# Seven slots for the spread C rows, extra TensorE products in two pauses, and last outputs in four banks

## What is computed

```python
# 1: c = x W + (x A_id) B_id
xp = c @ x_proj_w.T                        # 32 columns of dt_in, 16 of B, 16 of C
dt = softplus(dt_in @ dt_proj_w + dt_proj_b)
dA, dBx = exp(dt[..., None] * A), dt[..., None] * B * c[..., None]
h = dA_t * h + dBx_t                       # the scan over 64 steps, 16 states per feature
y = einsum('bdn,bn->bd', h, C_t)           # the states times C, summed over the 16 states
x = x + y + D * c
# 2: v = x W2 + bias + adapter;  logits = v @ router_w.T;  top 2 of 4 experts, softmax
x = x + gates * ((v @ A_e) @ B_e)          # "out": the last product, rank 64 to 1024 columns
```

## Time and profile before

| | us |
| --- | --- |
| median of 3 runs | 905.21 |
| the 3 runs | 905.06, 905.21, 910.86 |
| the profiled execution's own time | 910.61 |
| its span, first to last instruction | 908.40 |
| mean granted TensorE clock in the span | 0.968 of full |

### The profile page before, as it was taken

One profiled execution on the slowest core, in us unless ns is written; L12 is line 12 of the kernel. 1 busy time (PEld: TensorE's weight loads), 2 busy tenths in 40 slices (PEclk: granted clock), 3 DMA queues, 4 the chain that ended last, 5 costly groups with the idle time before them and its releaser, 6 DMA issues.

```text
span 908.4 us, 18640 instructions
## 1 busy us (share of the span) xinstructions
PE 808.6 (89%) x6416; PEld 770.8 (85%) x6416; DVE 764.3 (84%) x688; ACT 641.4 (71%) x1489; POOL 689.0 (76%) x349
## 2 busy tenths in 40 slices
PE   5999999999898989899987997889998999688784
PEld 4988998899888988899987997889987999577672
DVE  3447789989989898988997897989999799989993
ACT  4556778787677876787785875878777786768750
POOL 2015788898779886898887885889879888789791
PEclk9996999999999999999998999999999999789998
DMA  9988687575647667475647556485665653243211
GB/s 247 384 327 276 224 238 212 165 246 160 221 123 259 192 199 218 157 231 167 234 136 247 177 158 214 118 266 172 212 192 179 224 167 129 73 146 97 87 64 47
DMA packets 103113, 172.24 MB, mean 190 GB/s; under 512 B 21865, under 2 KB 71657, under 8 KB 94830
## 3 DMA queue, kind: packets, MB, share of 16 engines
q1 hardware_dynamic: 85614, 94.12, 34.7%
q10 hardware_dynamic: 17408, 76.95, 24.3%
HBM read 137.33 MB, written 33.69 MB: 188 GB/s over the span
## 4 chain that ended last, share of the span: by engine, by line
PE 56%; ACT 11%; DVE 10%; issue 8%; POOL 7%; DMA 5%; SPq 1%; POOLq 0%; ACTq 0%; DVEq 0%
PE jb L1047 25%; PE yp L1214 14%; PE dBx L1047 8%; DVE h L1011 6%; POOL hC L578 6%; ACT dA L612 6%; PE jb L1051 4%; PE yp L1047 3%; DMA stacked<-dtx_scratch 3%; POOL dtx L558 2%; DMA dtx_scratch<-HL 1%; DMA x<-in_x 1%; PE yp L1051 1%; DVE HL L906 1%; DVE Bd L829 1%
## 5 line engine op out<-in xcount | busy, mean ns | idle before, releaser
L578 POOL TENSOR_TENSOR hC<-h,Cb 128x1024 f32<-128x1024 f32 (+1 forms) x256 | 634.6, 2482 | 145.5 <-DVE h L1011 128.7
L1011 DVE TENSOR_TENSOR_SCAN h<-dA,dBx 128x1024 f32<-128x1024 f32 x256 | 583.2, 2280 | 67.8 <-PE dBx L1047 58.0
L612 ACT ACTIVATE dA<-dt,negA 128x252 f32<-128x252 f32 x1024 | 430.2, 494 | 75.2 <-DVE h L1011 64.9
L1214 PE MATMUL yp<-ident,hC 128*128 128x128 f32 x2048 | 274.9, 278 | 25.9 <-DVE dt L813 14.1
L1214 PEld LDWEIGHTS yp<-ident,hC 128*128 128x128 f32 x2048 | 237.0, 144 | 30.8 <-POOL hC L578 20.0
L1047 PE MATMUL jb<-xT,Wst 128*128 128x256 f32 x1416 | 213.9, 293 | 4.4 <-DVE dt L813 4.4
L1047 PE MATMUL dBx<-Bd,stacked 96*128 96x256 f32 x1024 | 187.3, 306 | 20.8 <-DMA stacked<-dtx_scratch 11.1
L1047 PEld LDWEIGHTS jb<-xT,Wst 128*128 128x128 f32 x1416 | 183.5, 192 | 7.1 <-DVE dt L813 5.2
L1047 PEld LDWEIGHTS dBx<-Bd,stacked 96*128 96x128 f32 x1024 | 147.3, 196 | 27.3 <-issue 24.4
L558 POOL TENSOR_TENSOR dtx<-dt,u 128x256 f32<-128x256 f32 x64 | 53.3, 834 | 40.0 <-DVE dt L813 40.0
L647 ACT ACTIVATE u<-jb 128x512 f32<-128x512 f32 x31 | 18.5, 598 | 41.1 <-PE jb L1047 38.7
(11 more groups left out here) (173 smaller groups left out, 721.7 us busy)
## 6 DMA issues: line engine op xcount, KB each, us to landing
Wst<-W_scratch ACTq DMA_DIRECT2D x54, 1024.0 KB, 5.7
stacked<-dtx_scratch SPq DMA_DIRECT2D x192, 128.0 KB, 2.7
dtx_scratch<-HL SPq DMA_DIRECT2D x64, 256.0 KB, 3.4
Cb<-c_scratch SPq DMA_DIRECT2D x32, 512.0 KB, 6.0
xres<-in_x SPq DMA_DIRECT2D x64, 128.0 KB, 3.9
out<-obuf SPq DMA_DIRECT2D x32, 256.0 KB, 3.3
xin<-in_x ACTq DMA_DIRECT2D x26, 256.0 KB, 5.0
GB<-in_L_cond_lora_B SPq DMA_DIRECT2D x64, 64.0 KB, 5.6
```

Of the source, the lines that this page charges most:

```text
L578: pool.tensor_tensor(*(x[:, :, ns, :] for x in times_C(un)), ALU.mult).then_inc(hC_made, 1)
L612: act.activation(dA[:, half % NDA, :].rearrange("p (b n t) -> p b n t", b=GB_, n=HS)[:, :, n, 1:STEPS], dt[:, j % NDT, :].rearrange("p (b ...
L1011: dve.tensor_tensor_scan(h[:, un % NH, :], dA[:, half % NDA, UNIT * p:UNIT * (p + 1)], dBx[un % 2][:, :], 0.0, ALU.mult, ALU.add).then_inc ...
L1214: last = pe.matmul(y, hC[:, un % NHC, P * n:P * (n + 1)], ident[:, :], is_transpose=True, start=un == 0 and n == 0, stop=False, skip_group ...
```

## The change

1. `Cb` gets seven slots in place of four. Unit un of group G lies in slot (4 G + un) mod 7. Where before the four spreads of a group were issued in (7, 1), (7, 2), (7, 3) of the group before and (0, 1) of its own, now two are issued in (6, 3), one in (7, 0) and one in (7, 1). The wait ahead of one is for the product that used the slot seven units' worth of C earlier.
2. A new helper `keep_clock(psum, n)` issues n products of 128 x 512 columns on `expBT` whose results nobody reads: 8 behind the setup, 9 ahead of gm and 2 behind it in the tail.
3. The eight products of the last group's outputs go into the four banks of `dBx`, in another order: both first products of outputs 0 and 1 need gm's high part alone, and the wait for the low part stands behind them. The additions are made in place in `x1`, and the last group's stores read from there; there is no wait for `out_done`.
4. A scratch of the program for software-made DMA descriptors goes from 1024 to 512 bytes.

```diff
+SPREAD = {(6, 3): (0, 1), (7, 0): (2,), (7, 1): (3,)}
-        Cb = sb("Cb", [P, UNITS, UNIT])
+        Cb = sb("Cb", [P, NCB, UNIT])
...
+        def C_slot(G, un):
+            return (UNITS * G + un) % NCB
...
             def spread_c(G, un):
                 if un == 0:
                     wait(sp_e, cscr_out, 64 * G + 64)
-                wait(sp_e, hC_made, UNITS * K * G - UNITS + un + 1)
+                s = UNITS * G + un - NCB
+                if s >= 0:
+                    sp_e.wait_ge(hC_made, UNITS * K * (s // UNITS + 1) - UNITS + s % UNITS + 1)
...
-                        if (j, un) == (0, 1) and not first:
-                            spread_c(G, UNITS - 1)
...
-                        if j == K - 1 and un >= 1 and not last:
-
-                            spread_c(G + 1, un - 1)
+                        for ahead in SPREAD.get((j, un), ()) if not last else ():
+                            spread_c(G + 1, ahead)
...
             for i in range(4):
-                job("out", i, G, G % 2, jb[i % 2])
+                half, tt = i // 2, i % 2
+                mine = x1[:, G % 2, tt, half * 512:(half + 1) * 512]
+                dve.wait_ge(full["out"], 4 * G + i + 1)
+                dve.tensor_tensor(mine, set_bank(i), mine, ALU.add).then_inc(taken["out"], 1)
...
+            def keep_clock(psum, n):
+
+
+                for _ in range(n):
+                    mm(psum, expBT[:, 0:P], expBT[:, 0:512], True, True)
...
             pe.wait_ge(set_taken, 5)
+            keep_clock(set_bank(3), 8)
...
-                                      ("gm", 0, "B", None), ("out", 0, "A", None), ("out", 1, "B", None), ("out", 2, "A", None),
-                                      ("out", 3, "B", None)):
+                                      ("gm", 0, "B", None)):
+                if name == "gm":
+                    keep_clock(yp[0][:, :], 9)
                 job(name, i, G, G % 2, jb["AB".index(bank)], bank, ks)
+            keep_clock(yp[0][:, :], 2)
+            pe.wait_ge(gm_hi, 2 * G + 2)
+            for i, part in ((0, 0), (1, 0), (0, 1), (1, 1), (2, 0), (2, 1), (3, 0), (3, 1)):
+                if (i, part) == (0, 1):
+                    pe.wait_ge(taken["gm"], G + 1)
+                last = mm(set_bank(i), gm[:, part, P * (i % 2):P * (i % 2 + 1)], expBT[:, 512 * (i // 2):512 * (i // 2 + 1)], not part, bool(part))
+                if part:
+                    last.then_inc(full["out"], 1)
```

More of the change, by code:

```diff
@@ L22 @@
 ROWS = 3 * Q
-NDA, NH, NHC, NDT = 2, 2, 4, 4
+NDA, NH, NHC, NDT, NCB = 2, 2, 4, 4, 7
 PARTS = ((0, 0), (0, 1), (1, 0))
@@ L211, in layer_kernel @@
                x1T[:, 4:8, :].rearrange("p k t -> p (k t)"), x1[:, 0, 0, :], x1[:, 0, 1, :], hC[:, 1, :], hC[:, 2, :], hC[:, 3, :]]
-        Wraw = [Cb[:, :, :].rearrange("p u c -> p (u c)").rearrange("p (k o) -> p k o", k=K // 2),
+        Wraw = [Cb[:, 0:UNITS, :].rearrange("p u c -> p (u c)").rearrange("p (k o) -> p k o", k=K // 2),
                 dA[:, :, :].rearrange("p h c -> p (h c)").rearrange("p (k o) -> p k o", k=K // 2)]
@@ L332, in set_bank, with times_C @@
             return dBx[i % 4 // 2][:, 512 * (i % 2):512 * (i % 2 + 1)]
-        def times_C(un):
+        def C_slot(G, un):
+            return (UNITS * G + un) % NCB
+        def times_C(G, un):
             return (hC[:, un % NHC, :].rearrange("p (n b t) -> p b n t", n=HS, b=2),
                     h[:, un % NH, :].rearrange("p (b n t) -> p b n t", n=HS, b=2),
-                    Cb[:, un, :].rearrange("p (b n t) -> p b n t", n=HS, b=2))
+                    Cb[:, C_slot(G, un), :].rearrange("p (b n t) -> p b n t", n=HS, b=2))
         def W_chunk(o):
@@ L413, in spread_c @@
                     wait(sp_e, cscr_out, 64 * G + 64)
-                wait(sp_e, hC_made, UNITS * K * G - UNITS + un + 1)
+                s = UNITS * G + un - NCB
+                if s >= 0:
+                    sp_e.wait_ge(hC_made, UNITS * K * (s // UNITS + 1) - UNITS + s % UNITS + 1)
                 src = c_scratch[G]
-                sp_e.dma_start(Cb[:, un, :], src[un:un + 1, :].to_broadcast([P, UNIT])).then_inc(C_in[un], 16)
+                sp_e.dma_start(Cb[:, C_slot(G, un), :], src[un:un + 1, :].to_broadcast([P, UNIT])).then_inc(C_in[un], 16)
             def put_dtx(G, i):
@@ L433, in store @@
                 half, tt = i // 2, i % 2
-                sp_e.dma_start(of_group(out_tok, G)[:, tt, half * 512:(half + 1) * 512], obuf[:, i % 2, :])\
+                of = slice(half * 512, (half + 1) * 512)
+                sp_e.dma_start(of_group(out_tok, G)[:, tt, of], x1[:, G % 2, tt, of] if G == GROUPS - 1 else obuf[:, i % 2, :])\
                     .then_inc(out_done[i % 2], 16)
@@ L577, in body @@
                         ns = slice(0, HS // 2 if s + 1 == UNITS * K * GROUPS else HS)
-                        pool.tensor_tensor(*(x[:, :, ns, :] for x in times_C(un)), ALU.mult).then_inc(hC_made, 1)
+                        pool.tensor_tensor(*(x[:, :, ns, :] for x in times_C(G, un)), ALU.mult).then_inc(hC_made, 1)
                         if (j, un) in DTX and not (final and DTX[j, un] >= K):
@@ L1028, in _ @@
             dve.wait_ge(C_in[UNITS - 1], 16 * GROUPS)
-            dve.tensor_tensor(*(x[:, :, HS // 2:, :] for x in times_C(UNITS - 1)), ALU.mult).then_inc(last_half, 1)
+            dve.tensor_tensor(*(x[:, :, HS // 2:, :] for x in times_C(G, UNITS - 1)), ALU.mult).then_inc(last_half, 1)
             add_residual(G, G % 2, K - 1, K * GROUPS - 1)
@@ L1331 @@
     from concourse.bass_utils import run_bass_kernel_spmd as _run
-    nc = _bacc.Bacc("TRN2", target_bir_lowering=False, num_devices=1, dynamic_dma_scratch_size=1024)
+    nc = _bacc.Bacc("TRN2", target_bir_lowering=False, num_devices=1, dynamic_dma_scratch_size=512)
     arrays, args = {}, []
```

## The result

The changed kernel is slower by 1.2%: 917.45 us (median of 13 runs, 912.54 to 924.49), beside 906.72 for the kernel before in the same measurement (13 runs, 899.48 to 920.27). The ratio is 1.0117, 95% interval 1.0089 to 1.0145. Ratios and intervals go by each kernel's fast executions, medians by all of them, so a ratio is not always the quotient of two medians. The profiled execution took 920.53 us, span 918.7, mean clock 0.961. The prediction was wrong in its sign: what its rival 4 describes came true, at six of the seven boundaries.

What follows compares the result with a forecast made beforehand. TensorE (89% busy) and VectorE (84%) trade places as the bound. From the median 905.2 - 2.8 - 3.0 - 2.2 + 0.4 - 2.4 = 895.2 us, as from the profiled 910.6 with 7.8 for 2.4; range 889 to 902.5.

Steps and rivals of the forecast that it cites:

- rival 4: At group boundaries the third spread delays the `stacked` loads, so scans wait and TensorE's clock falls: 922 us, chance 0.07.
- The third spread: Group boundaries: 512 KB C transfer ahead of `stacked` loads, mostly in a free stretch, costs 0.4 us, bounds 0 to 2.4.
- Code packets: Groups 2 and 4: 16 more instructions shift code fetches 1.1 us earlier, off slow puts; gains 7.8 us profiled, 2.4 median.
- Eight products: Behind the setup: unread products keep full clock through the first units; gains 2.8 us, bounds 0 and 3.4.
- Transposes and the clock: First unit: transposes do not keep the clock down; otherwise the gain of 2.8 us is nearer 1.6.
- The tail: Last outputs: unread products keep full clock, four banks and in-place additions remove waits; gains 3.0 us, bounds 0.9 and 3.1.
- Seven slots: Group 6: removes GpSimd's late wait for C; gains 2.2 us, bounds 0 and 2.2.
- Rival 3: C was on time in most groups and group 6's stall was chance, so slots change nothing: 897.4 us, inside forecast's 0.50.

Runs made afterwards that it cites:

- no_slots: The kernel before with the unread products and new tail alone, four slots and the spreads' old places: 904.77 us, ratio 0.9999 (0.9959 to 1.0039).

## Why the prediction was wrong, point by point

- **The third spread: the step that failed.** "A spread issued 0.4 us behind the put has its packets read while the put's landing is awaited, so mostly in a free stretch; I charge 0.4 us for all boundaries, bounds 0 and 2.4". It took 4.2 to 5.3 us to land and the loads came 2.0 to 3.0 us behind it, so they shared the engines with it. The six late boundaries took 2.8 to 7.4 us more than a clean one of 26.9; against the kernel before, where groups 4 and 6 were late too, the profiled sum rose by 21 us, and the median lies 16 us above the version with the spread behind the loads. The term of 0.4 us, at most 2.4, stands against that. My own figure for the slack, 1.8 us from landing to need, was not the fault; what I did not work out is that a third load delayed by up to two microseconds meets the weight load, issued 0.7 us behind it in the clear case, and then is not one but three to six late. Rival 4 had the wait and the lost clock, but not the weight load; that its 922 us lies near the 917.5 measured is partly luck, since it counted four boundaries of 5.7 us where there were six of 3.5 on average over the kernel before. Its chance of 0.07 was too low, since I weighed it by the spread's landing time alone.
- **Code packets, -7.8 from the profile and -2.4 from the median.** That they slow the puts they fall on is borne out by the 119 puts above, and inside the groups the profiled pair gained 8.9 us. The shift was mis-sized: 1.1 us forecast, but the packet at number 5's put moved from 0.44 to 0.05 us behind its issue in group 2 (put 2.90 to 2.48 us) and from 0.42 behind to 0.22 ahead in group 4 (2.97 to 2.29), and ahead of group 2 the packet at number 8 did not move clear (0.12 to 0.18). And I counted what clears and, of what is newly hit, only a bound of +2. I had listed the 64 puts and their packets; the same shift put a packet into number 8's put ahead of group 6, where none had been within 7 us (2.02 to 3.16 us). Measured net, with products of 8 columns: 0.9987 (0.9958 to 1.0017), no change seen.
- **Eight products, -2.8.** Right to scan (1, 0), where 3.6 us came; wrong beyond it. I ended the walk where the stretch at half clock ended, and did not ask when the weights land that the next unit needs. ScalarE's load of x now went out 3 us earlier (77.10 against 80.12) into the same DMA engines, and the weights landed 14.8 us behind the first scan, 12.3 before.
- **Transposes and the clock.** The window 71.2 to 84.8, full of transposes and pauses, ran at 1.00 in the changed kernel, but at 0.87 with the products alone and at 0.64 in no_slots, all with the same TensorE program there. Without the products it ran at 0.50 to 0.65 in four profiles. By "TensorE: Matmul & The Clock Gate", "Part 4: PE-mode transpose", of the Trainium skill, transposes don't count towards the full clock; here the clock held among them in some executions and fell in others, so neither my reading nor that rule alone forecasts this place.
- **The tail, -3.0.** 3.0 in the profile; 0.9944 (0.9906 to 0.9983) in the ratio, 1.5 to 8.5 us.
- **Seven slots, -2.2.** The C waits went, but no gain shows in the ratios: where the spreads are harmless, the version with them can't be told from the one without. The profiles have 0 to 2.2 us, the bounds I gave; 2.2 was the largest case and not the typical one. Rival 3 is not refuted and not shown.
- **Left open.** What no_slots is worth. By the ratio it is level with the kernel before (0.9999, 0.9959 to 1.0039) in spite of the tail's 3 us; by the medians it is 2.7 us below, which the tail alone would explain. By the profiles the products lost 2 us in the first chunks; the products alone measured 0.9973, and the intervals of these runs are too wide to add them up.

## What to carry to other kernels

A large transfer moved earlier in a queue must be placed against the small ones on the critical path: look at what is in flight when they are issued, and at which big transfer waits just behind them, since a small load that misses its gap shares the engines with a megabyte and loses several times its delay. Where a stall can be moved by instruction count alone, count what the same shift newly hits before booking the gain. An engine made faster in one place only helps up to the next load it needs: put that load first, then speed up the engine. The change without its item 1, with the first weights ahead, gave 897.5 us (ratio 0.9914, 0.9883 to 0.9945), which beats both kernels; the seven slots had no part in it. And read from the trace how far an edit has moved a DMA: four instructions later in the program were a quarter of a microsecond here.

## What was not expected of the hardware

- A queue's three loads of 128 KB, issued within 1.3 us, land 2.4 to 2.8 us after issue in a clear stretch. With a 512 KB transfer issued 2 to 3 us ahead of them, and a 1 MB transfer within 0.6 us of the third, the third took 5.6 to 8.8; with 512 KB ahead and no such weight load it took 3.9 to 4.6; with 128 KB ahead it took 2.6 to 2.7 wherever the put took under 2.6.
- Code packets of 16 KB, about 1.1 us of one DMA engine each, go with 256 KB puts of up to 3.9 us in place of 2.0 when they begin near the issue. The Trainium skill, "Runtime: NRT & Kernel Launch", "Instruction fetch mechanics", calls a block crossing mostly hidden; the cost that shows here is that of whoever waits for the put.
- Sixteen more instructions moved these packets, against the puts, by 1.2 us at one place (1.32 to 0.08 us behind number 8's put ahead of group 4), by 0.4 and 0.6 at number 5 of groups 2 and 4, and by nothing at number 8 ahead of group 2.
- Executions of one and the same kernel spread over 13 us in one measurement (898.3 to 911.8 for 24 of the kernel before) and over 21 in another (899.5 to 920.3 for 13), so one profile pair can show 10 us that the medians don't.
